# A token embedding, delta-rule attention and mixture-of-experts kernel: Internal layouts, transfer counts and the queue of two loads are changed

## The chip, the cores and the metric

The kernel runs on one core of one Trainium2 chip. The metric is the device time of one execution in microseconds (us); the figure given is the median of several runs. A profile comes from one more execution, and its time is given beside its span (first to last instruction).

## The reference

```python
h = embeddings[x]                                  # 8 x 512 tokens, 256 wide
a = layernorm(h)
k, q, v = conv4(a @ W.T + b) for each of k, q, v   # causal, 4 taps; v = silu(v)
k, q = k/|k|, q/|q|  per head;  eta = sigmoid(a @ Wbeta.T + bbeta);  b, v = eta*k, eta*v
for each chunk of the delta rule, 16 heads of 16:
    T   = tril(Bi @ Ki.T, -1);  inv = inverse(I + T);  Ui = inv @ (Vi - Bi @ W_t)
    W_new, W_avg_new = W_t + Ki.T @ Ui, running weighted average of the states
    O_i = Qi @ W_avg * a + Qi @ W_t * c + T_mat * (Qi @ Ki.T) @ Ui
h = h + rmsnorm(O) @ Wout.T + bout;  xn = layernorm(h)
out = h + shared SwiGLU expert(xn) + top-2 of 8 routed SwiGLU experts(xn), sigmoid gates
```

The reference takes chunks of 64 tokens, the kernel of C = 32. Everything is float32.

## The kernel before, in words

There are three stages. The five engines run programs of their own that wait for each other on semaphores; the order of work on each is written out by hand.

**Stage A** loops over the 8 batch rows b (512 tokens each). PE projects k, q and v (`project(b, 0)` to `project(b, 5)`, L575), ACT copies each out twice (`cv` L695, `raw` L698), DVE adds the other three taps (`tap`, L804). Norms, beta and transposes follow. `gram(b, half)` (L629) makes the Gram and score products, which DVE scales into `ng` and `sT` (L869, L874). SP stores q by channels (`qT_dram`, L471, 16 transfers a batch row), k by tokens (`kk_dram`, L477, 4), the Gram blocks (`n_dram`, L482, 4), beta times k and v (`bv_dram`, L486, 1; it waits for DVE's L815), then waits for its own Gram stores and loads them back turned (`nx`, L491), and stores the scores (`sT_dram`, L494). DVE inverts the blocks of batch row b-1 (`half_step`, L172 and L175) in the gaps of row b, and SP stores the inverse by `store_inverse` (L184, 8 transfers of 16 partitions each, in runs of 256 bytes).

From b = 3 on, PE, ACT, POOL and SP also work on **items**: an item r is one tile of 128 tokens, four items to a batch row, three rows behind. For item r, PE waits for `xbd` (the inverse, 4 transfers) and `bv_i` and applies the inverse (`apply_inverse`, L288); ACT copies the result out (`solved_out`: `yz_ch` L327, `y_out` L330); PE turns it (L299), ACT copies (`turned_out`, L337, L340), PE applies the scores `sbd` (`apply_scores`, L310), ACT copies (`scored_out`, L346, L349), PE turns (L320), ACT copies (`inner_out`, L354). POOL scales the queries `q_i` (L271) and adds (L276) in `sum_queries`. SP moves an item by `move_item(r)`: `load_x(r+1)` (waits for item r's L288), `store_y(r)`, `store_rest(r-1)`, `load_scores(r+1)` (waits for item r's L310 and L271). `xbd`, `sbd` and `q_i` have one buffer each, the outputs two. PE's order fixes where an item's steps stand between the projections: item 0's `apply_inverse` stands in front of `project(b, 1)`, item 1's in front of `project(b, 3)`. SP's order in a row is `move_item` of items 0 and 1, `store_inverse(b-2)`, `move_item` of item 2, the q, k, Gram and beta stores, `move_item` of item 3 between the Gram halves, `nx`, the scores.

**Stage B** has 32 steps s, each one chunk of 32 tokens of four batch rows. Before it SP stands still until all stores of stage A are in. `load_step(s)` loads `yy`, `zo`, `kk` and `qq`, 256 KB each, two steps ahead; PE takes `zo` in (`take_z`, L1040), adds state times y (`read_y`, L1051), grows the state (`grow`, L1082), and does the same for the output (`take_o`, `read_q`, L1069). The last 12 items run in steps 0 to 3, 5 to 8 and 12 to 15. The inverses of the last two batch rows end here too; they are stored after steps 3 and 11. Items 28 to 31 need the last one.

**Stage C** is the shared expert and the routed ones; the change does not touch it.

Loads in stage B as written before:

```python
sp.dma_start(zo[i][:].rearrange("p w d -> p (w d)"), zo_dram[c, b:b + GROUP].rearrange("b i x -> (b i) x"))
sp.dma_start(kk[i][:].rearrange("p n x -> p (n x)"), kk_dram[c, b:b + GROUP].rearrange("b i x -> (b i) x"))
```

With the chunk number in front in DRAM, the 128 rows of each are one even run.

## Time and profile before

| | |
|---|---|
| median of 3 runs | 1510.67 us (1509.09 to 1511.9) |
| profiled execution | 1518.6 us |
| its span | 1516.8 us |
| stage A | 0 to about 597 us |
| stage B | about 597 to 917 us |
| stage C | about 917 us to the end |
| PE, DVE, ACT, POOL busy | 78%, 50%, 34%, 26% of the span |
| SP's transfers | 202944 packets, 194.28 MB |

An engine's busy time says only how much it had to do; what ends an engine's idle time is said by the chain of waits. PE's share is an average over three stages with different limits.

### The profile page before, as it was taken

How to read it: one execution, taken by the hardware profiler on the slowest of the kernel's cores; microseconds unless marked ns; L12 is line 12 of the kernel's file. 1: busy time of each engine (PE TensorE's matmuls, PEld its weight loads, DVE VectorE, ACT ScalarE, POOL GpSimd, SP SyncE). 2: the span in 40 equal slices, each digit the busy share in tenths (PEclk: the TensorE clock that was granted, in tenths of full speed). 3: DMA queues.
4: the chain of work that ended last, by engine and by line, in shares of the span. 5: the costliest groups of instructions: out<-in, count | busy, mean ns of one | idle time of the engine just before them, and what ended most of it. 6: DMA issues, size and time to landing. Idle time of an engine off the chain costs nothing. (4 is left out here: it accounts for less than half of the span.)

```text
span 1516.8 us, 28805 instructions
## 1 busy us (share of the span) xinstructions
PE 1179.7 (78%) x10846; PEld 791.1 (52%) x10846; DVE 764.9 (50%) x1707; ACT 515.8 (34%) x1049; POOL 388.6 (26%) x366
## 2 busy tenths in 40 slices
PE   4766456566656561688697987999999999999997
PEld 2543334353535351466475764555666666666664
DVE  4599849586868683567646873221111212121211
ACT  3454245353636360433243332331122222222221
POOL 6100113131202021513226003662022222222222
PEclk9788679777878785867888997999999999999999
DMA  7644566868585968777687747953122323232322
GB/s 269 188 101 134 120 178 142 251 140 248 128 255 121 259 136 235 199 224 224 179 246 225 230 152 278 377 171 103 32 40 46 48 45 49 44 49 43 49 44 31
DMA packets 237366, 228.68 MB, mean 151 GB/s; under 512 B 88980, under 2 KB 177972, under 8 KB 236080
## 3 DMA queue, kind: packets, MB, share of 16 engines
q1 hardware_dynamic: 202944, 194.28, 45.3%
q0 software_dynamic: 16368, 19.96, 7.5%
q10 hardware_dynamic: 17920, 12.59, 2.8%
q8 instruction: 91, 1.49, 0.4%
q14 instruction: 43, 0.35, 0.1%
HBM read 117.39 MB, written 115.62 MB: 154 GB/s over the span
## 5 line engine op out<-in xcount | busy, mean ns | idle before, releaser
L1644 DVE TENSOR_TENSOR hid_all<-p_s,silu 128x512 f32<-128x512 f32 x103 | 71.3, 692 | 378.8 <-PE p_s L1495 249.7
L1694 POOL DMA_INDIRECT out_h<-y_sb,x_in x71 | 110.6, 1558 | 360.9 <-DVE y_sb L1656 343.0
L1552 ACT ACTIVATE silu<-p_m 128x512 f32<-128x512 f32 x103 | 61.5, 597 | 328.0 <-PE p_m L1488 223.4
L804 DVE SCALAR_TENSOR_TENSOR cv<-raw,conv_sb,cv 128x512 f32<-128x512 f32 x144 | 117.5, 820 | 83.6 <-ACT raw L698 81.7
L175 DVE TENSOR_TENSOR xt<-xt,prod 128x62 f32<-128x62 f32 (+15 forms) x248 | 142.0, 572 | 4.3
L172 DVE TENSOR_TENSOR prod<-nx,xt 128x62 f32<-128x62 f32 (+15 forms) x248 | 138.4, 558 | 2.5
L1510 PE MATMUL p_y<-wo,hid_all 128*128 x568 | 134.4, 379 | 0.8 <-ACT hid_all L1569 0.8
L1488 PE MATMUL p_m<-wi,xT_c 128*128 x284 | 133.5, 592 | 0.5 <-ACT xT_c L1565 0.5
L1495 PE MATMUL p_s<-ws,xT_c 128*128 x284 | 133.6, 593 | 0.0
L288 PE MATMUL p_item<-xbd,bv_i 128*32 128x128 f32 x1024 | 46.8, 340 | 108.4 <-issue 39.5
L575 PE MATMUL p_p<-xT,wqkv_sb 128*128 128x512 f32 x192 | 108.6, 705 | 0.7 <-issue 0.7
L1510 PEld LDWEIGHTS p_y<-wo,hid_all 128*128 128x128 f32 x568 | 102.5, 190 | 12.4 <-issue 1.4
L276 POOL TENSOR_TENSOR qy_out<-qy_out,sy_out 128x512 f32<-128x512 f32 x32 | 46.3, 1446 | 219.7 <-ACT sy_out L349 219.7
L271 POOL TENSOR_TENSOR qy_out<-q_i,cst_early 128x512 f32<-128x512 f32 x32 | 38.4, 1201 | 226.7 <-DMA q_i<-q_channels_dram 226.5
L288 PEld LDWEIGHTS p_item<-xbd,bv_i 128*32 128x32 f32 x1024 | 35.6, 135 | 116.7 <-issue 83.9
L629 PE MATMUL p_g<-kqM,kT 32*32 32x128 f32 x2048 | 52.8, 333 | 47.3 <-DVE h L874 26.4
L1684 POOL DMA_INDIRECT slots_in_dram<-rows,slot_of x64 | 62.2, 972 | 46.0 <-ACT rows L1560 31.5
L1488 PEld LDWEIGHTS p_m<-wi,xT_c 128*128 128x128 f32 x284 | 53.9, 190 | 38.4 <-issue 34.8
L1656 DVE COPY y_sb<-p_y 128x256 f32<-128x256 f32 x71 | 30.2, 425 | 85.5 <-PE p_y L1510 84.3
L629 PEld LDWEIGHTS p_g<-kqM,kT 32*32 32x32 f32 x2048 | 40.3, 121 | 59.0 <-issue 57.1
L1495 PEld LDWEIGHTS p_s<-ws,xT_c 128*128 128x128 f32 x284 | 48.5, 190 | 34.4 <-issue 34.4
L1453 PE MATMUL p_m<-xnT_c,wi 128*128 128x512 f32 x128 | 62.0, 608 | 5.3 <-DMA wo<-in_w_out 5.3
(155 smaller groups left out, 2093.9 us busy)
## 6 DMA issues: line engine op xcount, KB each, us to landing
slots_in_dram<-xt SPq DMA_DIRECT2D x18, 520.0 KB
x_in<-slots_in_dram SPq DMA_DIRECT2D x71, 130.0 KB, 2.1
q_channels_dram<-qT SPq DMA_DIRECT2D x128, 64.0 KB
k_tokens_dram<-h SPq DMA_DIRECT2D x32, 256.0 KB
chunk_gram_dram<-h SPq DMA_DIRECT2D x32, 256.0 KB
beta_kv_dram<-h SPq DMA_DIRECT2D x8, 1024.0 KB
nx<-chunk_gram_dram SPq DMA_DIRECT2D x8, 1024.0 KB, 6.3
scores_dram<-h SPq DMA_DIRECT2D x8, 1024.0 KB
```

What stands on the lines that cost most here:

```text
L172: ins = dve.tensor_tensor(pr, nx[b % 2][:, m, :, 0:m].rearrange("p e k -> p k e").unsqueeze(3).to_broadcast([P, m, 2, w]), xt[b % 2][:, m, ...
L175: ins = dve.tensor_tensor(kept, kept, pr, ALU.add)
L288: ins = pe.matmul(bank[C * f:C * f + C, n * P:(n + 1) * P], bv_i[r % 2][:, 4 * n + f, :], xbd[:, :, 4 * n + f, :], start=True, stop=True)
L575: ins = pe.matmul(p_p[n % 2][:], wqkv_sb[:, k, p, m * P:(m + 1) * P], xT[:, k, :], start=(k == 0), stop=(k == KH - 1))
L629: ins = pe.matmul(p_g[c * C:(c + 1) * C, g % 4, t % 2, g // 4, :], kT[r, g // 4, tok], kqM[r, g // 4, :, :, tok].rearrange("p w e i -> p ( ...
L804: ins = dve.scalar_tensor_tensor(cv[:, p, m, :], raw[:, p, m, j:j + L], conv_sb[:, p, m, j:j + 1], cv[:, p, m, :], ALU.mult, ALU.add)
L1488: ins = pe.matmul(p_m[n % 2][:], xT[s % 2][:, k, :], wi[:, e, k, :], start=(k == 0), stop=(k == KH - 1))
L1495: ins = pe.matmul(p_s[n % 2][:], xT[s % 2][:, k, :], ws[:, e, k, :], start=(k == 0), stop=(k == KH - 1))
L1510: ins = pe.matmul(p_y[s % 2][:, 0, :], hidT[s % 2][:, f * P:(f + 1) * P], wo[:, e, f, :], start=(f == 0), stop=(f == FK - 1))
L1644: dve.tensor_tensor(dst, p_s[n % 2][:], silu[n % 2][:], ALU.mult).then_inc(S["hid_ready"], 1)
L1684: pool.indirect_dma_start(xs_dram, bass.IndirectOffsetOnAxis(slot_of[:, t, k:k + 1], 0), rows[q][:, k, :], None).then_inc(s_scat[q], 16)
L1694: pool.indirect_dma_start(token_rows, bass.IndirectOffsetOnAxis(x_in[s % X_IN][:, D:D + 1].bitcast(U32), 0), y_sb[s % 2][:], None, compute ...
```

## The change

- `store_inverse` is one transfer of 128 partitions by 8 KB. `x_dram` keeps the solver's order, so each `xbd` load gathers 8 runs of 256 bytes for each of its 32 rows; before, a row was one run of 2 KB.
- The q stores are 8 transfers of 64 partitions by 2 KB instead of 16 of 16 partitions by 8 runs of 512 bytes; on the DRAM side each is 4 blocks of 16 rows. `q_i` is loaded in runs of 512 bytes; before, 2 KB.
- The k store is 1 transfer instead of 4, the store of z and inner 1 instead of 4, and y and the queries share one buffer `yq_out`, one store and one load `yq`. So `solved_out(r)` now waits for the joint store of item r-2, and that store waits for its queries.
- `kk_dram` and `zo_dram` are laid out by batch row. In stage B, `load_step` reads four batch rows' 32 tokens: 4 blocks of 32 rows of 2 KB, instead of 128 rows in one run. `yq` is issued behind the waits for u and o.
- `load_scores` (four `sbd` and one `q_i`) is issued by ACT, right behind `scored_out` in stage A and behind `inner_out` in stage B, with its waits.
- `load_x` stands a transfer earlier for each item: that of the next row's item 1 is now in front of the wait for the Gram stores; `store_item(r)` joins what `store_y` and `store_rest` did.

```diff
-    x_dram = nc.dram_tensor("chunk_inverse_dram", [B, L, H * C], F32, kind="Internal").ap()
+    x_dram = nc.dram_tensor("chunk_inverse_dram", [B, HP, NC_BATCH, C, ROW], F32, kind="Internal").ap()
-    qT_dram = nc.dram_tensor("q_channels_dram", [B, TILES, P, HQ, P], F32, kind="Internal").ap()
-    kk_dram = nc.dram_tensor("k_tokens_dram", [NC_BATCH, B, C, 2 * D], F32, kind="Internal").ap()
-    y_dram = nc.dram_tensor("y_channels_dram", [B // GROUP, NC_BATCH, P, GROUP, HQ * C], F32, kind="Internal").ap()
-    qy_dram = nc.dram_tensor("queries_dram", [B // GROUP, NC_BATCH, P, GROUP, HQ * C], F32, kind="Internal").ap()
-    zo_dram = nc.dram_tensor("z_and_inner_dram", [NC_BATCH, B, C, 2 * D], F32, kind="Internal").ap()
+    qT_dram = nc.dram_tensor("q_channels_dram", [B, HQ, P, L], F32, kind="Internal").ap()
+    kk_dram = nc.dram_tensor("k_tokens_dram", [B, L, 2 * D], F32, kind="Internal").ap()
+    yq_dram = nc.dram_tensor("y_and_queries_dram", [B // GROUP, NC_BATCH, P, GROUP, 2 * HQ * C], F32, kind="Internal").ap()
+    zo_dram = nc.dram_tensor("z_and_inner_dram", [B, L, 2 * D], F32, kind="Internal").ap()
...
-            for g in range(HP):
-                sp.dma_start(x_dram[b, :, g * ROW:(g + 1) * ROW].rearrange("(c k) x -> c k x", k=C),
-                             xt[b % 2][g * NC_BATCH:(g + 1) * NC_BATCH].rearrange("p k e i -> p k (e i)")
-                             ).then_inc(s_xst, 16)
+            sp.dma_start(x_dram[b].rearrange("g c k x -> (g c) (k x)"),
+                         xt[b % 2][:].rearrange("p k e i -> p (k e i)")).then_inc(s_xst, 16)
...
-                sp.dma_start(xbd[tok(c), c].rearrange("p h i -> p (h i)"), x_dram[b, t * P + c * C:t * P + (c + 1) * C]
+                sp.dma_start(xbd[tok(c), c].rearrange("p h i -> p (h i)"), x_dram[b, :, t * CH + c].rearrange("g k x -> k g x")
                              ).then_inc(s_x_in, 16)
             sp.dma_start(bv_i[r % 2][:].rearrange("p h x -> p (h x)"), bv_dram[b, t * P:(t + 1) * P]).then_inc(s_bv_in[r % 2], 16)
 
-        def load_scores(sp, r):
+        def load_scores(act, r):
             b, t = r // TILES, r % TILES
             if r:
-                sp.wait_ge(T["scored"], r)
+                act.wait_ge(T["scored"], r)
+            else:
+                act.wait_ge(T["zeroed"], 2)
+            act.wait_ge(s_st, STORES * (b + 1))
             for c in range(CH):
-                sp.dma_start(sbd[tok(c), c].rearrange("p h i -> p (h i)"), sT_dram[b, t * P + c * C:t * P + (c + 1) * C]
+                act.dma_start(sbd[tok(c), c].rearrange("p h i -> p (h i)"), sT_dram[b, t * P + c * C:t * P + (c + 1) * C]
                              ).then_inc(s_s_in, 16)
             if r:
-                sp.wait_ge(T["q_scaled"], r)
-            sp.dma_start(q_i[:], qT_dram[b, t]).then_inc(s_q_in, 16)
-
-        def store_y(sp, r):
-            b, t, i = r // TILES, r % TILES, r % 2
-            sp.wait_ge(T["y_ready"], r + 1)
-            sp.dma_start(y_dram[b // GROUP, t * CH:(t + 1) * CH, :, b % GROUP].rearrange("c p x -> p c x"),
-                         y_out[i][:].rearrange("p c n i -> p c (n i)")).then_inc(s_y_st[i], 16)
-
-        def store_rest(sp, r):
+                act.wait_ge(T["q_scaled"], r)
+            act.dma_start(q_i[:], qT_dram[b, :, :, t * P:(t + 1) * P].rearrange("n p l -> p n l")).then_inc(s_q_in, 16)
+
+        def store_item(sp, r):
             b, t, i = r // TILES, r % TILES, r % 2
             sp.wait_ge(T["z_ready"], r + 1)
             sp.wait_ge(T["inner_ready"], r + 1)
-            for c in range(CH):
-                sp.dma_start(zo_dram[t * CH + c, b], zo_out[i][tok(c)].rearrange("p w h d -> p (w h d)")
-                             ).then_inc(s_zo_st[i], 16)
+            sp.dma_start(zo_dram[b, t * P:(t + 1) * P], zo_out[i][:].rearrange("p w h d -> p (w h d)")).then_inc(s_zo_st[i], 16)
+            sp.wait_ge(T["y_ready"], r + 1)
             sp.wait_ge(T["q_ready"], r + 1)
-            sp.dma_start(qy_dram[b // GROUP, t * CH:(t + 1) * CH, :, b % GROUP].rearrange("c p x -> p c x"),
-                         qy_out[i][:].rearrange("p c n i -> p c (n i)")).then_inc(s_qy_st[i], 16)
-
-        def move_item(sp, r, more=True):
-            if more:
-                load_x(sp, r + 1)
-            store_y(sp, r)
-            if r:
-                store_rest(sp, r - 1)
-            if more:
-                load_scores(sp, r + 1)
+            sp.dma_start(yq_dram[b // GROUP, t * CH:(t + 1) * CH, :, b % GROUP].rearrange("c p x -> p c x"),
+                         yq_out[i][:].rearrange("p c w n i -> p c (w n i)")).then_inc(s_yq_st[i], 16)
 
...
             if r >= 2:
-                act.wait_ge(s_y_st[r % 2], 16 * (r // 2))
-            act.activation(y_out[r % 2][:].rearrange("p c n i -> p n c i"), bank[:].rearrange("p (n c i) -> p n c i", n=HQ, c=CH),
+                act.wait_ge(s_yq_st[r % 2], 16 * (r // 2))
+            act.activation(yq_out[r % 2][:, :, 0].rearrange("p c n i -> p n c i"), bank[:].rearrange("p (n c i) -> p n c i", n=HQ, c=CH),
...
                         if b >= AHEAD:
-                            move_item(sp, r)
-                            move_item(sp, r + 1)
+                            load_x(sp, r + 2)
+                            store_item(sp, r)
                         if b >= 2:
                             store_inverse(sp, b - 2)
                         if b >= AHEAD:
-                            move_item(sp, r + 2)
+                            load_x(sp, r + 3)
+                            store_item(sp, r + 1)
                         sp.wait_ge(s_nrm, b * 4 + 4)
...
+                        for n in range(HQ):
+                            for w in range(2):
+                                sp.dma_start(qT_dram[b, n].rearrange("(f w d) l -> w f d l", w=2, d=DH)[w],
+                                             qT[n % 2 * 4 * DH:(n % 2 + 1) * 4 * DH, n // 2]).then_inc(s_st, 16)
...
                                 if b >= AHEAD:
-                                    move_item(sp, r + 3)
+                                    load_x(sp, r + 4)
+                                    store_item(sp, r + 2)
+                        if AHEAD <= b + 1 < B and b >= AHEAD:
+                            load_x(sp, r + 5)
                         sp.wait_ge(s_ngst, 64 * (b + 1))
...
+                        if AHEAD <= b < B - 1:
+                            store_item(sp, r + 3)
                         if b == AHEAD - 1:
                             load_x(sp, 0)
-                            load_scores(sp, 0)
+                            load_x(sp, 1)
...
                         if c:
-                            sp.dma_start(yy[i][:].rearrange("p b n i -> p (b n i)"), y_dram[g, c].rearrange("p b x -> p (b x)")
-                                         ).then_inc(s_yy[i], 16)
-                        if s >= 2:
-                            sp.wait_ge(S["o_summed"], s - 1)
-                        sp.dma_start(zo[i][:].rearrange("p w d -> p (w d)"),
-                                     zo_dram[c, b:b + GROUP].rearrange("b i x -> (b i) x")).then_inc(s_zo[i], 16)
+                            sp.dma_start(yq[i][:].rearrange("p b w n i -> p (b w n i)"), yq_dram[g, c].rearrange("p b x -> p (b x)")
+                                         ).then_inc(s_yq[i], 16)
+                        sp.dma_start(zo[i][:].rearrange("p w d -> p (w d)"), zo_dram[b:b + GROUP, c * C:(c + 1) * C]
+                                     ).then_inc(s_zo[i], 16)
...
                             sp.dma_start(kk[i][:].rearrange("p n x -> p (n x)"),
-                                         kk_dram[c, b:b + GROUP].rearrange("b i x -> (b i) x")).then_inc(s_kk[i], 16)
+                                         kk_dram[b:b + GROUP, c * C:(c + 1) * C]).then_inc(s_kk[i], 16)
```

## Rows read from the trace of the kernel before

**Rows 1.** The page's busy tenths in 40 slices, each 37.9 us.

```profile
PE   4766456566656561688697987999999999999997
```

**Rows 2.** Windows: stretch, us, busy of PE, PEld, DVE, ACT, POOL, PEclk, DMA share, GB/s.

```profile
179.00:602.50 423.50, 232.51 (x3350) 168.41 (x3348) 310.68 (x578) 187.05 (x337) 76.81 (x66) 0.78 0.72 187
603.00:803.00 200.00, 152.66 (x2540) 117.86 (x2539) 119.89 (x327) 71.91 (x177) 70.54 (x62) 0.78 0.75 217
803.00:838.00 35.00, 28.26 (x482) 21.38 (x482) 23.85 (x77) 7.71 (x26) 23.30 (x28) 0.85 0.70 218
838.00:890.00 52.00, 49.80 (x988) 37.79 (x976) 42.67 (x162) 16.83 (x54) 0.00 (x0) 1.00 0.73 228
...
950.00:985.00 35.00, 35.00 (x107) 19.91 (x106) 7.93 (x12) 13.76 (x31) 22.44 (x32) 1.00 1.00 375
```

**Rows 3.** Waits of PE, 236 to 600 us: total us, times, longest.

```profile
PE p_item L288 <- issue: 38.5, 4, 14.1
PE p_item L288 <- DMA xbd<-chunk_inverse_dram: 31.4, 4, 8.5
```

**Rows 4.** Waits of DVE, 236 to 600 us.

```profile
DVE cv L804 <- ACT raw L698: 52.3, 11, 10.9
```

**Rows 5.** Timeline of SP, 401 to 438 us: start, us to issue.

```profile
401.16 11.71 SPq L471 DMA_DIRECT2D q_channels_dram<-qT  x16
412.97 3.73 SPq L477 DMA_DIRECT2D k_tokens_dram<-h  x4
...
419.50 0.97 SPq L486 DMA_DIRECT2D beta_kv_dram<-h  x1
420.57 3.51 SPq L225 DMA_DIRECT2D xbd<-chunk_inverse_dram  x4
...
430.02 1.06 SPq L482 DMA_DIRECT2D chunk_gram_dram<-h  x2
434.41 0.34 SPq L491 DMA_DIRECT2D nx<-chunk_gram_dram  x1
434.79 0.43 SPq L494 DMA_DIRECT2D scores_dram<-h  x1
435.33 2.17 SPq L225 DMA_DIRECT2D xbd<-chunk_inverse_dram  x4
```

**Rows 6.** Timeline, 425 to 453 us: PE and DVE around items 0 and 1.

```profile
427.61 1.94 PE L288 MATMUL p_item<-xbd,bv_i 128*32 128x128 f32 x32 [10.81 <-issue]
...
428.25 0.61 DVE L175 TENSOR_TENSOR xt<-xt,prod 128x440 f32<-128x440 f32 x1
...
438.62 0.75 DVE L804 SCALAR_TENSOR_TENSOR cv<-raw,conv_sb,cv 128x512 f32<-128x512 f32 x1 [1.51 <-ACT raw L698]
...
445.48 1.94 PE L288 MATMUL p_item<-xbd,bv_i 128*32 128x128 f32 x32 [7.85 <-DMA xbd<-chunk_inverse_dram]
```

**Rows 7.** Timeline of DVE, the same stretch.

```profile
452.56 0.75 DVE L804 SCALAR_TENSOR_TENSOR cv<-raw,conv_sb,cv 128x512 f32<-128x512 f32 x1 [10.72 <-ACT raw L698]
```

**Rows 8.** Timeline, 800 to 852 us: PE's steps 16, 20 and 21, an issue of ACT.

```profile
803.22 1.12 PE L1082 MATMUL p_w<-u,kk_b 32*128 32x64 f32 x32 [0.24 <-ACT u L1155]
...
839.47 0.52 ACTq L1197 DMA_DIRECT2D ffn_input_channels_dram<-xnT  x1
...
839.94 0.59 PE L1040 MATMUL p_u_turn_x<-zo,cst 128*128 128x256 f32 x2
...
845.76 0.59 PE L1040 MATMUL p_u_turn_x<-zo,cst 128*128 128x256 f32 x2
```

**Rows 9.** Timeline of PE and SP in stage B, where SP stores an inverse.

```profile
631.87 8.43 SPq L184 DMA_DIRECT2D chunk_inverse_dram<-xt  x8
...
646.58 1.93 PE L288 MATMUL p_item<-xbd,bv_i 128*32 128x128 f32 x32 [11.21 <-DMA bv_i<-beta_kv_dram]
...
758.55 1.22 PE L1040 MATMUL p_u_turn_x<-zo,cst 128*128 128x256 f32 x2 [9.67 <-DMA zo<-z_and_inner_dram]
```

**Rows 10.** Waits of SP, 236 to 600 us.

```profile
SPq L486 <- DVE h L815: 2.3, 3, 1.0
```

More of the change, by code:

```diff
@@ L196, in build @@
         yz_ch = sb(tail, "yz_ch", [P, HQ, P])
-        y_out = [sb(tail, f"y_out{i}", [P, CH, HQ, C]) for i in range(2)]
+        yq_out = [sb(tail, f"yq_out{i}", [P, CH, 2, HQ, C]) for i in range(2)]
         yz_tok = sb(tail, "yz_tok", [P, H, 2 * DH])
@@ L201, in build @@
         sy_out = [sb(tail, f"sy_out{i}", [P, CH, HQ, C]) for i in range(2)]
-        qy_out = [sb(tail, f"qy_out{i}", [P, CH, HQ, C]) for i in range(2)]
         s_st = tail.enter_context(nc.semaphore("kv_stored"))
@@ L206, in build @@
         s_s_in = tail.enter_context(nc.semaphore("item_scores_loaded"))
-        s_bv_in, s_y_st, s_zo_st, s_qy_st = ([tail.enter_context(nc.semaphore(f"{n}{i}")) for i in range(2)]
-                                                     for n in ("item_bv_loaded", "y_stored", "zo_stored", "queries_stored"))
+        s_bv_in, s_zo_st, s_yq_st = ([tail.enter_context(nc.semaphore(f"{n}{i}")) for i in range(2)]
+                                                     for n in ("item_bv_loaded", "zo_stored", "y_queries_stored"))
         T = {n: tail.enter_context(nc.semaphore("item_" + n)) for n in (
@@ L269, in sum_queries @@
             if r >= 2:
-                pool.wait_ge(s_qy_st[i], 16 * (r // 2))
-            pool.tensor_tensor(qy_out[i][:].rearrange("p c n i -> p n c i"), q_i[:].rearrange("p n (c i) -> p n c i", c=CH),
+                pool.wait_ge(s_yq_st[i], 16 * (r // 2))
+            pool.tensor_tensor(yq_out[i][:, :, 1].rearrange("p c n i -> p n c i"), q_i[:].rearrange("p n (c i) -> p n c i", c=CH),
                                table("q_scale")[:, t * P:(t + 1) * P].rearrange("p (c i) -> p c i", c=CH).unsqueeze(1).to_broadcast(
@@ L275, in sum_queries @@
             pool.wait_ge(T["sy_ready"], r + 1)
-            pool.tensor_tensor(qy_out[i][:], qy_out[i][:], sy_out[i][:], ALU.add).then_inc(T["q_ready"], 1)
+            pool.tensor_tensor(yq_out[i][:, :, 1], yq_out[i][:, :, 1], sy_out[i][:], ALU.add).then_inc(T["q_ready"], 1)
         def apply_inverse(pe, r, bank, alone):
@@ L680, in item @@
                     def item(b, k, step, bank):
+                        r = TILES * (b - AHEAD) + k
                         if b >= AHEAD:
-                            step(act, TILES * (b - AHEAD) + k, p_i[bank])
+                            step(act, r, p_i[bank])
+                        if b >= AHEAD and step is scored_out:
+                            load_scores(act, r + 1)
                     act.wait_ge(s_w, 16 * 7)
@@ L756, in _ @@
                         item(b, 3, turned_out, 1)
+                        if b == AHEAD - 1:
+                            load_scores(act, 0)
                     item(B - 1, 3, scored_out, 0)
@@ L930, in build @@
             s_lane = [sem(ctx, f"b_embedded_lanes{i}") for i in range(4)]
-            s_yy, s_qq, s_zo, s_kk, s_xn_out, s_xnT_out = (
+            s_yq, s_zo, s_kk, s_xn_out, s_xnT_out = (
                 [sem(ctx, f"b_{n}{i}") for i in range(2)]
-                for n in ("y_loaded", "q_loaded", "zo_loaded", "kk_loaded", "xn_stored", "xnT_stored"))
+                for n in ("yq_loaded", "zo_loaded", "kk_loaded", "xn_stored", "xnT_stored"))
             S = {n: sem(ctx, "b_" + n) for n in (
@@ L998, in _ @@
                             r = item_in[s - 1]
-                            move_item(sp, r, more=r + 1 < ITEMS and r != BREAK)
+                            more = r + 1 < ITEMS and r != BREAK
+                            if more:
+                                load_x(sp, r + 1)
+                            store_item(sp, r - 1)
                         if s == 11:
@@ L1002, in _ @@
                             load_x(sp, BREAK + 1)
-                            load_scores(sp, BREAK + 1)
                         if s == step_of[ITEMS - 1] + 2:
-                            store_rest(sp, ITEMS - 1)
+                            store_item(sp, ITEMS - 1)
                 @block.gpsimd
@@ L1046, in read_y @@
                             return
[L1047 removed]
+                        pe.wait_ge(s_yq[s % 2], 16 * q_loads(s))
                         pe.wait_ge(S["state_ready"], 2 * states(s - 1))
@@ L1221, in _ @@
                             inner_out(act, r, p_i)
+                        if r is not None and r + 1 < ITEMS and r != BREAK:
+                            load_scores(act, r + 1)
+                        if s == 10:
+                            load_scores(act, BREAK + 1)
                         if s >= 2:
```

40 lines of the change are left out of this document (14 added, 26 removed).

## Prediction

> **What bounds the kernel now.** I read the busy tenths first [rows 1]: PE is at nine tenths only from slice 22 on, which is stage C, and the change does not touch it. So the time is made or lost in the first 905 us. The windows by stage [rows 2] show that no engine is full in stage A with items (DVE 311 of 423.5 us), and that late in stage B (838 to 890 us) PE is busy 49.8 of 52 us while the DMA engines are busy 0.73 of the time.
>
> The waits of stage A say what ends PE's idle time: item loads. In 364 us PE stands 38.5 us in four waits and 31.4 us in four more, all in front of `apply_inverse` (L288) [rows 3]. DVE's idle time in the same stretch is 52.3 us at the tap, waiting for `raw` [rows 4]. The timeline shows where [rows 5, 6]: item 0's `xbd` is issued at 420.57, behind SP's 16 q stores (11.71 us), the k stores (3.73) and the beta store; PE starts at 427.61. Item 1's is issued at 435.33, behind `nx` and the scores, 1 MB each, and PE gets it at 445.48, ten microseconds later, for 10.72 us of idle DVE [rows 7]. In the first stall DVE works (its solver half-steps run to 428.25 + 0.61), so what sets the row's length is DVE, and only the second stall is worth its time.
>
> In stage B a step takes 5.82 us late (839.94 to 845.76), bound by PE [rows 8]. While items run it takes 11.8 us on average (step 16 grows its state at 803.22, so 17 steps in the 200 us before), and two steps stand 11.21 and 9.67 us because SP issues eight inverse stores for over 8 us in front of the loads [rows 9].
>
> **The change part by part, stage A.** SP loses, in a batch row with items, 7 of 8 inverse stores, 8 of 16 q stores, 3 of 4 k stores, 5 transfers for each item's outputs and 5 for each item's scores. That is time of SP, and it counts only where SP is what a stall waits for.
>
> *Item 0's stall.* Its load stands behind the beta store, which waits for DVE's L815. SP waits for DVE there in three of these rows already, 2.3 us in all [rows 10]; in the changed kernel it arrives earlier and waits for the same DVE. PE is idle, DVE is not; I count 0, but 3 us once (the row of 259 us, whose loads had the longest wait, 14.1 us). Together 3 us.
>
> *Item 1's stall.* The load now stands in front of `nx` and the scores, right behind item 0's L288 (429.5). The two loads need about 6 us there (as 420.57 to 427.6 needed 7.0), so `xbd` is in at 435.5 and PE, which is ready at 437.6 (445.48 less 7.85 of idle time), does not wait. But what is late next is the joint store: `solved_out` of item 1 now waits for y and the queries of the last row's item 3, and `store_item(r+3)` is issued behind `nx` and the scores, at about 433.5. Behind the same two transfers the load of before took 10.1 us; the joint store is 256 KB more and ACT's own loads run beside it, so it lands at 445 to 448. ACT stands there with `cv` and `raw` of projection 3 queued behind it, and DVE's tap starts at 447.5 to 450.5 instead of 452.56. ACT also issues five transfers for each item (0.52 us each by the nearest row [rows 8], 2.2 to 2.6 us), between `raw` 1 and `cv` 2, where DVE already waits 1.51 us [rows 6], and again in front of `cv` 5. This delays a tap by about 1 to 2 us before the wait, which absorbs it, and by up to 2 behind it. Net 2.5 us for each of four rows: 10 us, with bounds of -1 and 8 us each.
>
> *End of stage A.* SP issued the Gram stores of half 1 at 430.02, behind its moves of item 3, which begin at 420.57 and are now half as many transfers [rows 5]. In the last row this is on the path into stage B; I estimate 3 of these 9 us, since DVE has its second half ready not much earlier.
>
> *The stores of q.* They are half as many, of 2 KB runs; their first user is two rows later, so their price is the traffic in front of the Gram stores. If they run on few engines (below) they take 11 us where they took 11.71, and nothing moves.
>
> Stage A gives 3 + 10 + 3 = 16 us (bounds: 3 to 43, the upper one with all four second stalls gone and the first ones shorter).
>
> **Stage B.** SP's 8 us blocks and their two stalls go (up to 8 + 7 us). What comes in is the new shape of the `zo` and `kk` loads: before, 128 rows in one even run on both sides, now 4 blocks of 32 rows in DRAM against 128 partitions. No row of before shows a transfer whose outer count is under 16 on a side, so its price is bounded from both sides. Low: as before, 0. High: the transfer spreads over 4 of the 16 DMA engines, one for each block. Then each engine carries four times the share. From [rows 2], late stage B: 0.73 x 16 engines at 228 GB/s are 51.2 engine-us per MB; the fullest stretch, 1.00 x 16 at 375 GB/s, gives 42.7. `zo` and `kk` are 0.524 MB a step: 22.4 to 26.8 engine-us, so 5.6 to 6.7 us on each of four engines instead of 1.4 to 1.7. The rest of a step (228 GB/s x 5.82 us = 1.327 MB, less 0.524) is 2.1 to 2.6 us on every engine. Sum 7.7 to 9.3 us, against a step of 5.82 us.
>
> I take the high case. All transfers that run well in the trace of before (q from 16 partitions, the inverse by 16, rows by 32 or 128) have an outer count of 16 or more on both sides, so none speaks against it. The Trainium skill, "DMA: Bandwidth & Descriptors", section "Why a DMA increments its semaphore by 16 and not by 1", says that a DMA is split along each side's slowest dimension over the largest number of engines up to 16 that divides both counts; by that rule 4 and 128 give 4 engines, and by it the q stores (4 against 64) get 4 as well. The same page's rule that transfers should be fewer and larger would speak for the change; no run here shows yet which weighs more.
>
> *Late steps.* Step 20 to step 30, 10 steps: with 8.5 us (the middle of 7.7 and 9.3) instead of 5.82, 27 us; the steps 16 to 19, four in 35 us [rows 2] and so over 8 us each anyway, 2 us. Together 29 us (19 to 37).
>
> *Steps with items.* The stretch of 200 us has a DMA share of 0.75: 150 us on each engine [rows 2]. About 31 loads of `zo` and `kk`, 8.1 MB, at three sixteenths more per engine: 65 to 78 us. Sum 215 to 228 us on the four engines. They can't be full, since items wait for each other's loads; the stalls that go are already in this count, because it goes by work and not by time. At 215 to 228 of work with some 5% of idle time the stretch takes 226 to 240: I take 230, 30 us more (15 to 53, the upper end with a tenth of idle time). ACT's five issues per item, 12 times 2.2 us, lie in this slack; if the stretch were not bound by DMA, they would cost up to half, 13 us.
>
> **Sum.** -16 + 29 + 30 = +43 us. The profiled execution took 1518.6 us, 1.8 more than its span and 7.9 more than the median; added to it this gives 1561.6, and on the median 1510.67 + 43 = 1554 us.
>
> **The rivals.**
> *The loads spread as before (faster).* Nothing in the trace excludes it. Then stage A gives its 16 us, the two stalls of stage B give 15, the shorter SP queue about 5 more and ACT's issues take 3: 1510.67 - 33 = 1478 us (1460 to 1492). It decides as soon as a `zo` load lands in about 3 us.
> *Four engines, but covered.* If packets on four engines run at the fastest rate and stage A gains its upper bound, the sum is -43 + 19 + 15 = -9: 1502 us (1492 to 1520). Against it: 7.7 us is over 5.82 at the best rate seen.
> *Four engines, and the queue stands behind them.* If SP's later transfers wait until the slow ones are through, the cycle from o to the next load gets the whole 9.3 us plus a landing, some 11 us a step: 10 x 5.2 + 53 + 10 for the steps 16 to 19 = +115, less 8 for stage A: 1618 us.
>
> **How the numbers follow.** The forecast, 1520 to 1600, 0.68; spread as before 0.16; covered 0.09; standing queue 0.07. For 8 in 10 the range holds the forecast and the covered case: 1490 to 1605. The likeliest alone is 1520 to 1600. Within 0.2% (3 us) is about what a measurement can't tell from no change. Faster takes the spread case and two thirds of the covered one, 0.22; same 0.04; slower 0.74.
>
> **What would show it.** Stage A: no wait of PE for item 1's `xbd`; in its place ACT's `yq_out` copy late in items 1, near 445 us. Stage B: a late step of 7.7 to 9.3 us with PE waiting for `zo` or `kk`, and a DMA share there that falls although the engines used are full (16 engines are averaged): about 0.5. Wrong: steps of 5.8 us late in stage B mean the loads spread; a stage A that grows means ACT's waits cost more than SP's stalls did.

## The result, and the profile after

The changed kernel takes 1545.67 us (median of 4 runs, 1540.7 to 1548.88) against 1509.92 us (median of 4, 1509.09 to 1511.9) for the kernel before: a ratio of 1.0232, 95% interval 1.0197 to 1.0267. It is slower by 2.3%. The prediction had 1554 us and slower.

The profiled execution has a span of 1546.8 us, 30.0 more than before. These moments in both timelines say where they went: the first `take_z` (end of stage A), and `grow` of steps 0, 16, 20 and 30. From the first `take_z` to `grow` of step 0 it is 3.0 us in all three columns. The last column has the same for the run in which the blocks of 32 rows are taken apart (below).

| stretch | before | after | difference | after, loads in even rows |
|---|---|---|---|---|
| start to first `take_z` | 602.5 | 601.4 | -1.1 | 594.5 |
| grow 0 to grow 16 | 197.7 | 209.1 | +11.4 | 191.8 |
| grow 16 to grow 20 | 32.6 | 33.3 | +0.7 | 27.8 |
| grow 20 to grow 30 (10 steps) | 58.4 | 76.4 | +18.0 | 58.2 |
| grow 30 to the end of the span | 622.6 | 623.6 | +1.0 | 621.4 |

By this table stage A gave nothing back, and stage B lost 30 us. But the first `take_z` already waits for a load in the new form. SP issues the first `zo` load, and PE starts with it, before the change at

```profile
599.42 0.36 SPq L982 DMA_DIRECT2D zo<-z_and_inner_dram  x1
602.54 1.19 PE L1040 MATMUL p_u_turn_x<-zo,cst 128*128 128x256 f32 x2 [31.48 <-DMA zo<-z_and_inner_dram]
```

and after it at

```profile
594.46 0.58 SPq L970 DMA_DIRECT2D zo<-z_and_inner_dram  x1
601.39 1.19 PE L1027 MATMUL p_u_turn_x<-zo,cst 128*128 128x256 f32 x2 [31.53 <-DMA zo<-z_and_inner_dram]
```

So stage A proper ends 5.0 us earlier, and the first load of blocks takes 6.9 us instead of 3.1, which costs 3.8 of them. `e1_rows32` and `e9_scores_b_sp` (below) have the same stage A and even rows: there the first `zo` load is issued 8.3 and 11.4 us earlier than before, and lands in 3.4 us. So stage A gives 5 to 11 us, with that scatter between profiles of the same code.

The page (DMA queues) shows that the packets did fall, from 237366 in all:

```profile
DMA packets 207725, 228.64 MB, mean 148 GB/s; under 512 B 82636, under 2 KB 155244, under 8 KB 205416
q1 hardware_dynamic: 150264, 177.47, 36.0%
q10 hardware_dynamic: 40960, 29.38, 6.6%
```

q10 is ACT's queue. The windows of stage B (steps 0 to 16, and the late steps) answer to [rows 2]:

```profile
604.00:813.00 209.00, 163.71 (x2517) 126.12 (x2506) 115.44 (x324) 70.13 (x175) 65.34 (x58) 0.74 0.67 210
846.00:923.00 77.00, 63.07 (x1124) 45.61 (x1124) 49.78 (x184) 19.82 (x62) 0.00 (x0) 0.93 0.54 176
```

Late in stage B a step takes 7.64 us where it took 5.82, and the DMA share falls from 0.73 to 0.54: the engines look emptier while the kernel waits for them. Hardly any wait of PE there bears the name of a DMA (0.8 us over the window); the longest in total, and some rows of the timeline, read

```profile
PE p_w L1069 <- issue: 6.4, 8, 1.2
...
861.79 1.12 PE L1069 MATMUL p_w<-u,kk_b 32*128 32x64 f32 x32 [0.43 <-issue]
...
866.55 0.67 PE L1027 MATMUL p_u_turn_x<-zo,cst 128*128 128x256 f32 x2 [0.47 <-ACT xnT L1180]
...
869.34 0.90 PE L1069 MATMUL p_w<-u,kk_b 32*128 32x64 f32 x24 [0.82 <-issue]
```

L1069 is `grow`, the reader of `kk`. The experiments show that this "issue" is the wait for the key rows.

How many DMA engines a load uses can be counted in the trace's own packets. `zo` and `kk` move in packets of 2 KB, and to every transfer belong some packets of 4 bytes, which come at its end. Before the change SP's queue has about 64 of these small packets in a late step, 16 for each of its four loads. In the changed kernel it has 24: 16 for `yq`, and 4 each for `zo` and `kk`. The 2 KB packets say the same: while the first `zo` and `kk` loads are under way, up to 18 of them are in flight at once before the change, and for most of the time just 4 in the changed kernel. So a load of 4 blocks runs on 4 engines; and as `zo` and `kk` together keep 4 packets in flight and not 8, both have the same 4.

In stage A the waits from 236 to 600 us (of PE, ACT and DVE, each answer cut to the rows used) answer to [rows 3, 4]:

```profile
PE p_item L271 <- DMA xbd<-chunk_inverse_dram: 39.9, 4, 11.4
PE p_g L615 <- ACT kqM L732: 25.5, 5, 5.5
...
ACT yq_out L313 <- DMA y_and_queries_dram<-yq_out: 19.2, 4, 5.5
ACT kqM L732 <- issue: 18.3, 5, 4.0
...
DVE cv L795 <- ACT raw L687: 31.6, 13, 5.0
...
DVE h L860 <- PE p_g L615: 15.3, 5, 5.0
```

Item 1's stall on PE is gone, as the change meant. DVE's wait at the tap fell from 52.3 to 31.6 us. But DVE has a new wait of 15.3 us for the Gram products (L615), where before it had 0.2. The timeline of ACT shows how it comes about, and what stands in front of item 1's copy of y:

```profile
398.96 1.50 ACTq L233 DMA_DIRECT2D sbd<-scores_dram  x2
399.38 0.69 ACT L332 ACTIVATE sy_out<-p_item,cst_early 128x512 f32<-128x512 f32 x1
400.49 1.74 ACTq L233 DMA_DIRECT2D sbd<-scores_dram  x2
402.27 1.37 ACTq L237 DMA_DIRECT2D q_i<-q_channels_dram  x1
403.69 2.56 ACT L732 ACTIVATE kqM<-qT,cst_early 128x512 f32<-128x512 f32 x4 [3.62 <-issue]
...
446.99 0.69 ACT L313 ACTIVATE yq_out<-p_item,cst_early 128x512 f32<-128x512 f32 x1 [3.97 <-DMA y_and_queries_dram<-yq_out]
```

The first five rows: ACT copies item 2's scored result out and must issue item 3's five transfers, 4.6 us, before it makes the masked queries that the Gram products need. The last row: the copy waits for the joint store of the last row's item 3, whose issue is in SP's timeline at 435.56, behind `nx` and the scores:

```profile
431.07 2.40 SPq L221 DMA_DIRECT2D xbd<-chunk_inverse_dram  x4
433.51 0.45 SPq L223 DMA_DIRECT2D bv_i<-beta_kv_dram  x1
434.01 0.43 SPq L475 DMA_DIRECT2D nx<-chunk_gram_dram  x1
434.48 0.43 SPq L478 DMA_DIRECT2D scores_dram<-h  x1
435.01 0.45 SPq L243 DMA_DIRECT2D z_and_inner_dram<-zo_out  x1
435.56 0.40 SPq L246 DMA_DIRECT2D y_and_queries_dram<-yq_out  x1
```

### The profile page after: what moved, and what is told of

Same layout as the page of the kernel before. It is cut to its first block and busy times, and to the rows that moved or that the text cites. A ratio compares the mean times of both kernels' runs of the same rounds, so it can differ in the third digit from the quotient of the medians.

```text
span 1546.8 us, 28590 instructions
## 1 busy us (share of the span) xinstructions
PE 1201.0 (78%) x10846; PEld 806.6 (52%) x10846; DVE 765.1 (49%) x1707; ACT 515.1 (33%) x1049; POOL 388.1 (25%) x366
## 5 line engine op out<-in xcount | busy, mean ns | idle before, releaser
L171 DVE TENSOR_TENSOR prod<-nx,xt 128x62 f32<-128x62 f32 (+15 forms) x248 | 134.4, 542 | 2.5
L259 POOL TENSOR_TENSOR yq_out<-yq_out,sy_out 128x512 f32<-128x512 f32 x32 | 45.0, 1406 | 240.4 <-ACT sy_out L332 240.2
L615 PE MATMUL p_g<-kqM,kT 32*32 32x128 f32 x2048 | 52.7, 358 | 61.9 <-ACT kqM L732 32.4
L254 POOL TENSOR_TENSOR yq_out<-q_i,cst_early 128x512 f32<-128x512 f32 x32 | 39.0, 1220 | 227.2 <-DMA q_i<-q_channels_dram 162.9
L615 PEld LDWEIGHTS p_g<-kqM,kT 32*32 32x32 f32 x2048 | 42.9, 130 | 70.3 <-issue 67.5
L684 ACT ACTIVATE cv<-p_p,now_b,conv_sb 128x512 f32<-128x512 f32 x48 | 37.4, 780 | 89.6 <-PE p_p L561 83.5
```

What stands on the lines that cost most here:

```text
L171: ins = dve.tensor_tensor(pr, nx[b % 2][:, m, :, 0:m].rearrange("p e k -> p k e").unsqueeze(3).to_broadcast([P, m, 2, w]), xt[b % 2][:, m, ...
L615: ins = pe.matmul(p_g[c * C:(c + 1) * C, g % 4, t % 2, g // 4, :], kT[r, g // 4, tok], kqM[r, g // 4, :, :, tok].rearrange("p w e i -> p ( ...
```

## The experiments

Each run is compared with the kernel before on the same chip. The medians of the kernel before were 1513.27 us in the first group, 1505.08 in the second and 1505.53 in the third, so ratios are compared, not microseconds. The first group holds `e1`, `e2`, `e3` and `e5`, the second `e4`, `e6`, `e7` and `e9`, the third the rest, each on a chip of its own. Executions of one kernel scatter by up to 22 us, so single profiles tell a stretch to several us at best: stage A, up to its last Gram product, has the same code in the changed kernel, in `e1_rows32` and in `e9_scores_b_sp`, and ended it at 569.3, 565.4 and 561.2 us.

**Blocks taken apart: `e1_rows32`.** For `zo`, and in the same way for `kk` (the waits of PE four times as high):

```diff
-sp.dma_start(zo[i][:].rearrange("p w d -> p (w d)"), zo_dram[b:b + GROUP, c * C:(c + 1) * C]
-             ).then_inc(s_zo[i], 16)
+for j in range(0, GROUP, 1):
+    sp.dma_start(zo[i][j * C:(j + 1) * C].rearrange("p w d -> p (w d)"),
+                 zo_dram[b + j, c * C:(c + 1) * C]).then_inc(s_zo[i], 16)
```

> The changed kernel, in which every load of a stage B step of the z/inner rows and of the key rows is four transfers of 32 even rows each in place of one of 4 blocks of 32 rows; the layout in DRAM stays the new one. Theory (the block form keeps 12 of the 16 DMA engines idle): the late step falls from 7.64 us back to 5.8 to 6.2 us, the stretch of steps 0 to 16 from 209 to about 198 us, and the whole to 1505 to 1520 us. Rival 1 (the layout in DRAM, the joint load of y and queries, or the order of the loads makes the step long): the late step stays at 7.5 us or above and the whole at 1545. Rival 2 (SP's six more issues of 0.5 us a step weigh): the late step lies between 6.2 and 7.5 us, with SP busy without a gap.

Measured: 0.9948 (0.9908 to 0.9988), 1504.03 us. The late step is 5.82 us, with eight transfers in place of two. The window of ten late steps:

```profile
817.00:875.00 58.00, 55.56 (x1120) 42.45 (x1121) 47.79 (x180) 18.42 (x60) 0.00 (x0) 1.00 0.72 225
```

The loss of stage B is the blocks', whole. The layout, the joint load of y and queries and the six more issues cost nothing there that shows. A late step now has about 140 of the 4-byte packets on SP's queue, near the 144 of nine transfers with 16 each.

**Two blocks to a transfer: `e2_rows64`.** The same with `j` in steps of 2 and two transfers of 64 rows.

> The changed kernel, with each of the same loads as two transfers of 2 blocks of 32 rows. A dose of the theory that the number of blocks sets how many DMA engines a transfer uses: with two engines to a transfer the late step is 8 to 15 us (8 if the two transfers fall on different engines, 15 if on the same) and the whole is 1550 to 1720 us. Rival (the size of a transfer or its count matters, not its blocks): the late step lies between that of one transfer and that of four even ones, 6 to 7.6 us, and the whole between 1515 and 1545 us.

Measured: 1.1038 (1.1004 to 1.1072), 1668.92 us. Late steps take 12.3 us. Window of ten late steps, and PE's wait there:

```profile
926.00:1049.00 123.00, 80.41 (x1120) 58.88 (x1120) 48.36 (x180) 18.93 (x60) 0.00 (x0) 0.76 0.32 108
```

```profile
PE p_w L1071 <- issue: 39.6, 10, 4.8
```

Twice the number of transfers, half the blocks in each, and the step goes from 7.64 to 12.3 us with a DMA share of 0.32: what counts is the number of blocks in a transfer, not its size or count. 12.3 us lies between the two values expected. The packets decide between them: a step has 24 of 4 bytes (16 for `yq`, 2 for each of the four others), and at most two of the 2 KB packets are in flight for 94% of the time, so all four transfers use the same two engines. The 3.96 us in front of `grow`, ten times, is named "issue" here as well. Each of these ten `grow` starts 0.39 to 0.44 us behind a 4-byte packet, and 3.7 to 4.9 us after ACT made `u`: the name hides the wait for `kk`.

**The blocks alone on the kernel before: `e3_blocks_alone`.** `kk_dram` and `zo_dram` as `[B, L, 2 * D]`, the stores as before, and

```diff
-zo_dram[c, b:b + GROUP].rearrange("b i x -> (b i) x")).then_inc(s_zo[i], 16)
+zo_dram[b:b + GROUP, c * C:(c + 1) * C]).then_inc(s_zo[i], 16)
-kk_dram[c, b:b + GROUP].rearrange("b i x -> (b i) x")).then_inc(s_kk[i], 16)
+kk_dram[b:b + GROUP, c * C:(c + 1) * C]).then_inc(s_kk[i], 16)
```

> The kernel before, with only the new layout in DRAM of the z/inner rows and of the key rows and their loads of 4 blocks of 32 rows; all stores keep their count and all else is as it was. Theory: this one part holds the whole loss of stage B, so the late step is 7.4 to 8 us where it was 5.8 and the kernel is 25 to 35 us slower than before (1535 to 1545 us). Rival (another part of the change, such as the joint load of y and queries, or the scores' loads on ACT's queue, holds it): the late step stays under 6.2 us and the time within 5 us of before.

Measured: 1.0261 (1.0205 to 1.0317), 1553.23 us; late step 7.55 us, steps 0 to 16 207.9 us (+10.2).

```profile
853.00:928.00 75.00, 64.74 (x1109) 46.90 (x1113) 48.56 (x180) 19.32 (x60) 0.00 (x0) 0.89 0.54 175
```

This one part costs as much as the whole change. The two halves multiply to it: 1.0261 x 0.9948 = 1.0208, inside the interval of 1.0232.

**The scores back on SP: `e5_scores_sp`.** ACT's calls go, and SP has, for each item of stage A (and likewise in stage B):

```diff
 load_x(sp, r + 2)
+load_scores(sp, r + 1)
 store_item(sp, r)
```

> The changed kernel, with the items' scores and queries issued by SP again, behind the inverse loads of the item after. Theory (ACT's five issues in front of the masked queries keep the Gram products and DVE waiting in stage A): the mask copies of the queries run 3.6 us earlier in each of the last 5 batches, DVE's 15.3 us of waits for the Gram products go, stage A ends about 10 us earlier (between 588 and 596 us), and with stage B as it is in the changed kernel the whole is about 1536 us, or less if ACT's 40.7 us of issue gaps in steps 0 to 16 also set the end there (to 1525 us). Rival (SP's queue takes the wait over, since the score loads now stand in front of the Gram loads, or other waits stand right behind): stage A ends within 3 us of 601 us and the whole at 1540 to 1548 us.

Measured: 1.0542 (1.0507 to 1.0577), 1594.29 us. Both accounts were wrong. Stage A ends at 657.8 us, 56 later. PE's waits from 236 to 590 us:

```profile
PE p_item L293 <- DMA sbd<-scores_dram: 128.5, 12, 19.8
```

SP now runs one inverse load further ahead, and `load_x(r + 2)` waits for item r + 1 to be solved. Whatever follows it on SP can't be issued earlier; the scores of item r + 1, which are needed right after it is solved, come 10.7 us late each time. So with the inverse loads in this order, the scores need a queue other than SP's, and ACT's gives them one; that belongs on the change's credit side. Whether they could stand on SP in front of `load_x` was not tried.

**The layout by chunk: `e4_old_kk_zo`.** `kk_dram` and `zo_dram` by chunk as before, with four stores and one load of 128 even rows each; all else as changed.

> The changed kernel, with the key rows and the z/inner rows laid out by chunk as before: four stores of 32 partitions for each, one load of 128 even rows for each in stage B. Theory (even rows use all DMA engines, the count of transfers matters less): late step 5.8 us, the whole within 5 us of the run with four transfers of 32 even rows, which was at 0.995 of before. If the saved 6 issues of 0.5 us a step on SP matter in the item stretch, steps 0 to 16 are a few us shorter than its 192 us; if the 15 more stores a batch in stage A matter, stage A ends 3 to 8 us later than its 594.5 us. Rival (the layout itself matters beside the spread): late step over 6.2 us.

Measured: 0.9957 (0.9927 to 0.9986); late step 5.82 us, steps 0 to 16 187.1 us, stage A ends at 592.2. The same as four transfers of 32 rows, within the noise: only even rows matter.

The next seven keep the loads in 32 even rows, unless the text says otherwise.

**An earlier store: `e6_store_early`.**

```diff
-if AHEAD <= b + 1 < B and b >= AHEAD:
+if AHEAD <= b < B - 1:
+    store_item(sp, r + 3)
     load_x(sp, r + 5)
 ...
-if AHEAD <= b < B - 1:
-    store_item(sp, r + 3)
```

> The version with four transfers of 32 even rows, and in stage A the store of the batch's last item moved in front of the inverse load, the Gram reload and the scores' store, so that it is issued some 5 us earlier. Theory (ACT's wait of 18.8 us over 4 batches for the joint store, at the copy of y of item 1, holds the projections behind it and so DVE): the wait goes, and stage A ends 10 to 18 us earlier than 594.5 us, the whole near 1490 us. Rival (the wait is slack: the projections behind it wait for PE or DVE anyway, or the reload of the Gram rows that now stands behind the store is late): the wait goes but stage A ends within 4 us of 594.5 us and the whole stays at 1500 to 1508 us.

Measured: 0.9829 (0.9793 to 0.9865), 1476.34 us; stage A ends at 576.2 us. ACT's wait for the store is gone from the list of 236 to 575 us, and DVE's, from 31.6 us at the tap, reads

```profile
DVE cv L794 <- ACT raw L686: 13.5, 8, 2.8
DVE h L859 <- PE p_g L614: 11.7, 5, 3.3
```

A call moved by 5 us of queue time is worth 1.2% (0.9829 over 0.9948, each to about 0.4%). The base was measured on the first group's chip; on this one two other kernels with even rows and without the edit, `e4` and `e9`, gave 0.9957 and 0.9955.

**Later score loads: `e7_scores_late`.**

```diff
-if b >= AHEAD and step is scored_out:
+if b >= AHEAD and step is scored_out and k != 2:
     load_scores(act, r + 1)
 ...                                  # behind the four mask copies of the queries
+if b >= AHEAD:
+    load_scores(act, TILES * (b - AHEAD) + 3)
```

> The version with four transfers of 32 even rows, and in stage A ACT's five issues for item 3 moved behind the mask copies of the queries. Theory (the 17.5 us of ACT's issue gap in front of these copies delays the Gram products and DVE): DVE's 15 us of waits for the Gram products go, stage A ends 8 to 15 us earlier than 594.5 us, the whole near 1492 us. Rival (the issues only move to another place of ACT's order, and item 3's scores land later and hold PE): stage A ends within 4 us of 594.5 us, the whole at 1500 to 1508 us.

Measured: 0.9873 (0.9837 to 0.9908), 1484.8 us; stage A ends at 578.6 us. DVE's waits, same stretch:

```profile
DVE cv L797 <- ACT raw L687: 28.5, 12, 4.8
...
DVE h L862 <- PE p_g L615: 0.2, 1, 0.2
```

The wait for the Gram products is gone and the one at the tap hardly moved. In this profile steps 0 to 16 took 200.3 us, 8.5 more than in the run without the edit, though their code is the same; from 186.8 to 200.3 us were seen over the versions with even rows. What sets this stretch's phase was not found.

**Both: `e8_both`.**

> Both edits of stage A together on the version with four transfers of 32 even rows: the early store of the batch's last item (alone at 0.983 of before) and ACT's five issues behind the mask copies (alone at 0.987, the base at 0.995). Theory (two separate gaps on ACT): the gains add, 0.975 to 0.980 of before, about 1468 to 1474 us, and stage A ends near 565 us. Rival (the same slack is given back only once): 0.981 to 0.985, stage A ends at 573 to 577 us.

Measured: 0.9780 (0.9756 to 0.9804), 1471.73 us; stage A ends at 568.9 us. The sum of the two gains would be 0.9755, just outside the interval but itself known to half a per cent: they add, nearly or fully.

```profile
DVE cv L796 <- ACT raw L686: 14.6, 7, 4.2
...
DVE h L861 <- PE p_g L614: 0.2, 1, 0.2
```

**Score loads on SP in stage B alone: `e9_scores_b_sp`** (without the two edits). ACT's `load_scores` of stage B go, and SP calls them behind `store_item(sp, r - 1)`.

> The version with four transfers of 32 even rows, and in stage B alone the items' scores and queries issued by SP again, behind the store of the item before. Theory (in steps 0 to 16 ACT stands 42.8 us in its issues before it can copy u, on which the recurrence hangs): steps 0 to 16 fall from 192 us by 10 to 20 us, the whole to 1485 to 1495 us. Rival (SP, with 9 loads of a step, 5 of the inverse and 5 of the scores, is late with the next step's rows, or the stretch is bound by PE's and ACT's work and the gap is slack): 188 to 200 us for the stretch and 1500 us or above for the whole.

Measured: 0.9955 (0.9933 to 0.9977), 1498.02 us; steps 0 to 16 take 194.2 us: nothing gained. ACT's 42.8 us of issue gaps in front of `u` did go; PE's first wait there is now

```profile
PE p_u_turn_x L1032 <- DMA zo<-z_and_inner_dram: 12.3, 4, 8.8
```

for rows that SP issues late. The gap had moved from one queue to the other. So this run does not say what ACT's issues cost, only that SP can't take them for less.

**The old layout with both edits: `e10_both_old_layout`.**

> Both edits of stage A together, on the version with the key rows and z/inner rows laid out by chunk as before (at 0.996 of before without them). Theory (SP has room in both stages, so the two ways to even rows are worth the same): within 0.3 per cent of the same two edits with four transfers of 32 even rows. Rival: SP's 15 more stores a batch in stage A cost again once ACT no longer waits, and this is 5 us or more slower; or its 6 fewer issues a step in stage B pay, and it is 5 us or more faster.

Measured: 0.9817 (0.9795 to 0.9840), 1475.55 us: 0.4% behind `e8_both`, with intervals that just overlap. The profiles don't show why (stage A ends at 571.9, steps 0 to 16 take 190.7 us), so it stays open whether the 15 more stores a batch cost.

**The q stores: `e11_both_q16`.** 16 transfers of 16 even rows each for 8 of 4 blocks of 16.

```diff
-for n in range(HQ):
-    for w in range(2):
-        sp.dma_start(qT_dram[b, n].rearrange("(f w d) l -> w f d l", w=2, d=DH)[w],
-                     qT[n % 2 * 4 * DH:(n % 2 + 1) * 4 * DH, n // 2]).then_inc(s_st, 16)
+for f in range(4):
+    for m in range(2):
+        for w in range(2):
+            sp.dma_start(qT_dram[b, m::2, f * C + w * DH:f * C + (w + 1) * DH].rearrange("n d l -> d n l"),
+                         qT[m * 4 * DH + f * DH:m * 4 * DH + (f + 1) * DH]).then_inc(s_st, 16)
```

> Both edits of stage A on the version with four transfers of 32 even rows, and the queries stored in 16 transfers of 16 even rows in place of 8 of 4 blocks of 16 rows. Theory of the prediction (the block form of the q stores is covered and costs nothing, while 8 more issues of SP are covered too): within 3 us of the same kernel with 8. Rival 1 (the 8 block stores use 4 engines and stand in front of later loads, as in stage B): 5 to 15 us faster, in stage A alone. Rival 2 (SP's 8 more issues, 4 us a batch, delay the key rows' and Gram stores): 5 to 20 us slower over 8 batches.

Measured: 0.9778 (0.9758 to 0.9799), 1471.38 us: no difference. The block stores do run on few engines: in the changed kernel, from 397.7 to 408 us, four of their 2 KB packets were in flight for more than half of the time and hardly ever more. They are not without a price in the queues either. Over the whole trace a block store took SP 0.89 us to issue in `e8_both` and an even one 0.51 us here, and ACT's score loads of stage A took 0.73 us each there and 0.52 here. None of this reaches the whole time: either it is covered, or a gain from even rows and a loss from eight more issues cancel.

**Item 0's inverse earlier: `e12_x_early`.** `load_x(sp, r + 4)` moved from behind the beta store to in front of the wait for the beta rows.

> Both edits of stage A on the version with four transfers of 32 even rows, and the inverse load for the next batch's item 0 moved in front of the wait for the beta rows, where SP stands 7 us with the buffer already free. Theory (PE's 40 us of waits over 4 batches for this load hold ACT's copies and then the projections): the waits of 10 us each fall to 3 to 5 us, and stage A ends 8 to 20 us earlier than without it. Rival (in this stretch PE and ACT only wait for DVE, which is the bound, so an earlier item 0 is slack): the waits fall but the time stays within 4 us.

Measured: 0.9793 (0.9769 to 0.9816), 1472.82 us: no gain. PE's waits from 236 to 565 us, and ACT's, say why:

```profile
PE p_item L271 <- DMA xbd<-chunk_inverse_dram: 14.9, 5, 6.4
...
PE p_item L271 <- issue: 8.9, 3, 4.0
...
ACT yq_out L313 <- DMA y_and_queries_dram<-yq_out: 12.5, 6, 4.5
```

PE's 40.8 us in `e8_both` fell to 14.9, or to 23.8 with the 8.9 named "issue", and stage A ended only 2.2 us earlier. The wait was slack, and 12.5 us came back on ACT: the copies, now early, stand for the joint store again.

## Why the prediction was right, and where its sizes were off

The total, 1554 against 1545.67 us (43 more against a measured 36), is right in sign, and the cause that it names, few engines for loads in blocks, is the one that the runs show. That it came so near is in part luck: all three of its terms are too far out (-16, +29, +30 against -1.1, +18.7, +11.4 in the trace), and the error of the first offsets about half of the other two.

*Late steps, +27 for ten.* Right mechanism, size +18.0. The step was put at 7.7 to 9.3 us, used 8.5, measured 7.64. The working by engine time comes nearest at its lower end, where a MB costs the 42.7 engine-us of the fullest stretch: 0.524 MB on four engines 5.6 us, the rest 2.1, sum 7.7. With two engines the same sum gives 11.2 + 2.1 = 13.3 us; `e2_rows64` measured 12.3. The middle of the range was the wrong choice, and the trace shows why the price fell: SP's 2 KB packets took 105 ns each in a late step before, 90 ns in the changed kernel and 85 in `e2_rows64`, which is 51, 44 and 41 engine-us per MB. A packet was quicker where fewer engines carried the load. The rule of the Trainium skill that was weighed, "DMA: Bandwidth & Descriptors", section "Why a DMA increments its semaphore by 16 and not by 1" (as many engines, up to 16, as divide both slowest dimensions), agrees with the three doses here: 32 even rows 5.82 us, 4 blocks 7.64, 2 blocks 12.3, with 16, 4 and 2 of the 4-byte packets to a transfer.

*Steps 16 to 19, +2.* Measured +0.7.

*Steps with items, +30.* Measured +11.4, below the lower bound of 15. The term that was mis-sized is the work of the four engines, "215 to 228 us", with 5% and more of idle time added: the whole stretch took 209. The window's row splits it. A DMA share of 0.67 over 209 us is 140 us on an average engine, where the forecast took over the 150 of before. The 31 loads are 3968 packets, at 90 ns 357 engine-us, so they add 67 us to each of the four, as at the forecast's low rate (65). The sum is 207 us, and the stretch took 2 more, not 11 or 12. By this sum the four engines were busy nearly all the time; it is an estimate, since packets of different queues overlap on an engine (the same sum for a late step gives 8.4 us in 7.6). For the size of the effect there are two runs. `e3_blocks_alone` has the blocks at +10.2 on the kernel before; taking them out of the changed kernel (`e1_rows32`) gave 17.3. The versions with even rows differ by 13 us here with the same code, so the two agree no better than 10 to 17.

*ACT's issues in stage B* were said to lie in slack, or to cost up to 13 us otherwise. That stays open. With even rows, `e9_scores_b_sp` moved them to SP and gained nothing, because SP has no room for them either. With blocks, `e5_scores_sp` has them on SP too and took 197.8 us for steps 0 to 16, 11.3 less than the changed kernel; that is within the same scatter.

*Stage A, -16.* Measured -1.1 to the first `take_z`, of which the first block load had taken 3.8 back; to the issue of that load it is -5.0, and -8.3 and -11.4 in the two other profiles of this code. So 5 to 11 us are missing. The steps of it:
- Item 0's stall counted at 3 us once, since DVE and not PE sets the row: right. `e12_x_early` took 17 to 26 us of PE's wait away and gained nothing.
- Item 1's stall goes and the joint store takes its place, landing at 445 to 448 us: right to the place, the copy starts at 446.99. The prediction left this wait in place and counted only what stays beside it. `e6_store_early` shows that it was worth 1.2%, some 18 us, and hung on the order of a few calls of SP.
- "ACT also issues five transfers for each item ... This delays a tap by about 1 to 2 us": this is the step that failed. It looked at items 0 and 1, where ACT's issues fall between projections. Item 2's fall in front of the mask copies of the queries (L732), where PE and then DVE wait: 3.62 us in 403.69's row, 18.3 us over five batches, 15.3 us of DVE. `e7_scores_late` prices it at 0.75% (to about half a per cent), 11 us, and ended stage A 16 us earlier in its profile. That is as much as is missing or more, so without it stage A would have given about what was forecast.

*The q stores, "nothing moves".* Right for the whole time, by `e11_both_q16`. Their issue was put at 11 us on few engines and takes 7.54 (the changed kernel at 397.72).

*The rival "the loads spread as before", 1478 us*, had its own test in `e1_rows32`: 0.9948, so 33 us forecast, 8 measured (20 between the two profiles). It lacked in stage A, as above, and in stage B, where steps 0 to 16 gave 5.9 us against a forecast of 17 from stalls, queue and ACT's issues. That `e8_both` then gains 33.8 us comes from its two edits and not from these terms.

*Signs.* PE without a wait for item 1's `xbd`, ACT's late copy near 445, a step near 7.7 and a DMA share near 0.5: all seen. "PE waiting for `zo` or `kk`" was seen at the first `take_z` by its name, and late in stage B under another, "issue".

The best version found, `e8_both` (with `e11_both_q16` beside it), is 2.2% faster than before and takes 33.8 us less; against the changed kernel that is 0.9780 over 1.0232, or 4.4%.

## What to carry to other kernels

Merging transfers saves issues on a queue and can cost on the engines: look at the slowest dimension of each side of a merged transfer, and price it as its bytes over the engines that the blocks leave (here the rate of the fullest stretch came nearest); then ask whether anybody waits for it. Count the packets in flight to see how many engines a transfer really uses: the average DMA share hides it. Where issues are moved to a computing engine, go through every place at which they are called and name what that engine does next. And when a stall is moved, move the thing it now waits for as well: here two moved calls were worth three times what the merging gave with even rows (0.9780 over 0.9948, against 0.9948).

## What the runs showed of the hardware that I had not expected

- A wait for a transfer can stand as "issue". In `e2_rows64` it is 39.6 us over ten steps, each ended by a landing packet 0.4 us before; no such wait is among PE's in `e1_rows32`, where only the loads' shape differs.
- Two loads of 4 blocks in one queue did not spread over eight engines: both ran on the same 4, by the 4 packets in flight for both together (2 in `e2_rows64` for four transfers). In late steps this left the average DMA share at 0.54 and 0.32 while the kernel waited for the loads.
- A late DMA costs clock too. Ten late steps of the same work kept PE busy for 55.56 us at a granted clock of 1.00 (5.82 us a step), 63.07 us at 0.93 (7.64 us) and 80.41 us at 0.76 (12.3 us). The clock's records in these stretches know only two levels, 1.2 and 2.4 GHz; in the changed kernel some 10 of the 77 us are at the lower one, in `e2_rows64` about half of the time, and PE waits in nearly every step of both. Of the 19 us that the window of the changed kernel is longer, 7.5 are PE's busy time and 11.5 its idle time. How much of the 7.5 would have fallen in slack was not told apart.
- An issue can be slow. In the rows shown ACT's took 0.75 to 1.37 us each, five of them 4.6 us, where five on SP took 2.9 (431.07 to 433.96). The engine isn't what makes the difference: in the changed kernel from 236 to 600 us ACT's issues took 0.52 us on average while SP issued nothing, and 0.86 while it did, SP's own 0.56 and 0.94. With q stores of even rows (`e11_both_q16`) ACT's score loads fell from 0.73 to 0.52, so the block stores on SP's queue have a part in it; how they do it is open.
